# Issuing the products of probabilities and values for two key blocks together in a macaron attention kernel

## The reference, cut to what matters

```python
x = x + 0.5 * ffn(layernorm(x))      # one 128x128 product on inputs rounded to 4-bit floats in blocks of 32
x = x + attn(layernorm(x))           # 16 heads of 8 features, 512 x 512 scores for each head
x = x + 0.5 * ffn(layernorm(x))

def attn(x):
    xq, xk, xv = x @ wq.T + bq, x @ wk.T + bk, x @ wv.T + bv     # then split into heads, rotary on q and k
    scores = einsum('bhqd,bhkd->bhqk', q, k) / sqrt(8)
    return einsum('bhqk,bhkd->bhqd', softmax(scores), v)
```

## Time and profile before

| | us |
|---|---|
| median of 3 runs | 546.12 |
| lowest and highest | 543.88, 546.65 |
| the profiled execution, whole | 543.84 |
| its span, first to last instruction | 542.0 |

### The profile page before, as it was taken

One profiled execution on the slowest core, in us unless ns is written; L12 is line 12 of the kernel. 1 busy time (PEld: TensorE's weight loads), 2 busy tenths in 40 slices (PEclk: granted clock), 3 DMA queues, 4 the chain that ended last, 5 costly groups with the idle time before them and its releaser, 6 DMA issues.

```text
span 542.0 us, 8359 instructions
## 1 busy us (share of the span) xinstructions
PE 455.4 (84%) x2564; PEld 151.8 (28%) x2564; DVE 439.3 (81%) x1004; ACT 380.4 (70%) x746; POOL 228.5 (42%) x336
## 2 busy tenths in 40 slices
PE   2140799999979999999989998999899989998841
PEld 1120232332323332333233222323233323232211
DVE  6636789897999789987998799979997798898125
ACT  6557138687876788687877777878777786777730
POOL 8100047423755365536562665447543624012300
PEclk9985679999999999999999999999999999999995
DMA  5012411231122202231122212210322023200000
GB/s 163 20 48 85 137 41 51 86 95 50 29 91 73 84 31 79 70 101 49 50 89 89 70 51 89 90 66 24 103 74 90 23 76 100 60 2 2 21 1 19
DMA packets 27960, 34.86 MB, mean 64 GB/s; under 512 B 6278, under 2 KB 21260, under 8 KB 27916
## 3 DMA queue, kind: packets, MB, share of 16 engines
q1 hardware_dynamic: 26284, 33.94, 20.3%
q10 hardware_dynamic: 1632, 0.39, 0.3%
HBM read 21.34 MB, written 8.39 MB: 55 GB/s over the span
## 4 chain that ended last, share of the span: by engine, by line
PE 53%; DVE 27%; issue 7%; ACT 6%; POOL 3%; DMA 2%; SPq 1%; POOLq 0%; ACTq 0%; DVEq 0%
PE ot L1105 16%; DVE negmax L882 14%; PE sc L1092 14%; PE st L1081 12%; ACT probs L638 3%; PE misc L1030 3%; PE misc L1047 2%; PE misc L1070 2%; DVE stats_f L751 1%; DVE amax_f L774 1%; ACT feat_k L528 1%; PE misc L1055 1%; PE misc L1025 1%; DMA feat_k<-parts_k 1%; PE misc L1063 1%
## 5 line engine op out<-in xcount | busy, mean ns | idle before, releaser
L882 DVE TENSOR_REDUCE negmax<-sc 128x1 f32<-128x512 f32 x512 | 331.4, 682 | 50.7 <-PE sc L1092 50.1
L638 ACT ACTIVATE probs<-st 128x512 f32<-128x512 f32 x512 | 271.7, 602 | 80.2 <-PE st L1081 78.7
L1092 PE MATMUL sc<-feat_k,feat_q 96*128 96x512 bf16 x512 | 185.3, 391 | 14.7 <-DVE negmax L882 11.7
L1081 PE MATMUL st<-feat_q,feat_k 99*128 99x512 bf16 x512 | 158.1, 380 | 9.6 <-ACT probs L638 8.9
L1105 PE MATMUL ot<-probs,vfeat 128*32 128x512 f32 x1024 | 136.2, 604 | 1.1 <-ACT probs L638 1.0
L1092 PEld LDWEIGHTS sc<-feat_k,feat_q 96*128 96x128 bf16 x512 | 49.7, 97 | 162.3 <-DVE negmax L882 105.7
L1081 PEld LDWEIGHTS st<-feat_q,feat_k 99*128 99x128 bf16 x512 | 49.3, 98 | 82.6 <-ACT probs L638 55.9
L1014 PE MATMUL misc<-identb,xq_f 128*128 128x128 bf16 x64 | 6.8, 235 | 36.9 <-DVE xq_f L826 36.5
L406 POOL TENSOR_TENSOR rstd_f<-ve_f,nhalf 128x4 f32<-128x4 f32 x16 | 16.5, 1034 | 40.8 <-DVE nm_f L763 40.7
L447 POOL TENSOR_SCALAR maxparts<-negmax 128x16 bf16<-128x16 f32 x32 | 8.3, 258 | 57.6 <-DVE negmax L882 57.6
L1105 PEld LDWEIGHTS ot<-probs,vfeat 128*32 128x32 f32 x1024 | 20.2, 108 | 37.5 <-ACT probs L638 23.7
(11 more groups left out here) (134 smaller groups left out, 468.8 us busy)
## 6 DMA issues: line engine op xcount, KB each, us to landing
feat_q<-parts_q SPq DMA_DIRECT2D x96, 96.0 KB
feat_k<-parts_k SPq DMA_DIRECT2D x96, 96.0 KB
qkswap<-qkpre SPq DMA_DIRECT2D x32, 128.0 KB, 2.0
parts_q<-qkparts_q SPq DMA_DIRECT2D x24, 128.0 KB, 2.3
parts_k<-qkparts_k SPq DMA_DIRECT2D x24, 128.0 KB, 2.3
xres<-in_L_attn_x_dram SPq DMA_DIRECT2D x8, 256.0 KB, 5.5
out_dram<-xres SPq DMA_DIRECT2D x8, 256.0 KB, 2.5
feat_q<-maxrows ACTq DMA_DIRECT2D x32, 12.0 KB
```

Source lines behind the costliest of these rows:

```text
L638: nc.scalar.activation(probs[:, s % US, j * S:(j + 1) * S], st[:, bank(2 * s + j), :], ACT.Exp, scale=SCALE).then_inc(exp_done, 1)
L882: nc.vector.tensor_reduce(negmax[:, g, j:j + 1], sc[:, bank(16 * g + j), :], AX.X, ALU.max, negate=True).then_inc(sc_maxed, 1)
L1081: nc.tensor.matmul(st[:, bank(2 * s + j), :], feat["k"][par][0:MROWS, h, kb * P:(kb + 1) * P], feat["q"][par][0:MROWS, h, :], start=True, ...
L1092: nc.tensor.matmul(sc[:, bank(16 * g + j), :], feat["q"][par][0:SROWS, h, t * P:(t + 1) * P], feat["k"][par][0:SROWS, h, :], start=True, s ...
```

## The change

`times_v` is called twice in a row in every fourth step, in place of once in every second: in step 3 of a unit for key blocks 2 and 3 of the unit before, in step 7 for key blocks 0 and 1 of the present unit. Key blocks 2 move from step 1 to step 3, and key blocks 0 from step 5 to step 7; blocks 3 and 1 stay. The matmuls, their operands and their order among themselves are the same, and so are all waits.

```diff
             def slot(b, par):
                 for s in range(STEPS):
                     mb, mpar, mg, ms = ahead(b, par, s)
-                    if s % 2 == 1:
-                        kb = (s % US // 2 + 2) % T
-                        vb, vpar, vg = unit_from(b, par, s // US, -1 if kb >= 2 else 0)
+                    if s % 4 == 3:
+                        half = s % US // 4 ^ 1
+                        vb, vpar, vg = unit_from(b, par, s // US, -half)
                         if has(vb):
-                            times_v(vb, vpar, vg, kb)
+                            times_v(vb, vpar, vg, 2 * half)
+                            times_v(vb, vpar, vg, 2 * half + 1)
                     if has(mb):
                         scores(mb, mpar, mg, 2 * ms)
```

## The result

The changed kernel takes 576.56 us (median of 4 runs, 576.16 to 577.63) against 545.09 for the kernel before on the same chip; the ratio is 1.058, with a 95% interval from 1.055 to 1.061. The forecast was 564.5 with a range of 548 to 576. The direction was right, the size was not: the profiled spans differ by 575.1 - 542.0 = 33.1 us where the sum had said 18.6.

A forecast was written before the change was run, and what follows sets the result against it. No engine alone was taken as the bound: TensorE, VectorE and ScalarE couple through two three-bank queues. Six full batches at +2.4 us (14.6) plus 4 for the last two gave +18.6, forecast 564.5 us, range 548 to 576.

The forecast's parts named there:

- TensorE's saving of 0.23 us a merge: Each joining of two `times_v` blocks removes 0.23 us of TensorE; 63 of them, 14.5 us if all on the path.
- The sign that I gave for it: TensorE's busy time in the profile after would be lower, by some 10 us or more.
- The bare cycle, +0.2: Four-step stretch without other work: later `sc` matmuls wait for maxima to free banks, 5.88 us instead of 5.68.
- Cycles 1, 3, 4, 6, 7 and 8: Four-step stretches of a middle batch: 1 and 7 unchanged, 3 +0.87, 4 -0.45, 6 +0.65, 8 +0.1 us.
- Cycle 5: Fifth four-step stretch: `sc` of step 22 waits for a maximum behind four `stats`, 7.06 against 6.40 us, +0.65.
- Cycle 2, +0.6: Second four-step stretch: the whole double block follows the wait for `turn_max`, 7.66 against 7.05 us.
- Batches 6 and 7, +4: Last two batches, no projections ahead and fewer feed-forward steps: 16 cycles lose about 0.25 us each, 4 us.
- The rival "slower by more": Every cycle's block finds both readers empty and their idle times add, up to +30: 576 us; within slower's 0.83 chance.
- The rival "faster": Each merge's 0.23 us lies on the path and readers keep up: 531.6 us, or 538.9 for half; chance 0.10.
- The rival "no change": Losses of cycles 2, 3, 5 and 6 are partly given back in the next cycle and cancel: 546 us; chance 0.07.

The follow-up runs named there:

- the light kernels: Kernels before and after, each with maxima and exponentials taken of 256 of 512 columns: 527.62 us (before) and 538.68 us (after).
- four repeats: Kernel after with the second `sc` matmul of step 9 issued five times instead of once: 572.26 us, ratio 1.053.
- the step moved: Kernel after with GpSimd's third part of k in step 9 instead of 8: 568.31 us, ratio 1.045; with repeated matmuls as well, 568.04 us.

## Why the prediction was right in direction and wrong in size

- **TensorE's saving of 0.23 us a merge**: right. It appears in full in the light kernels' cycles 1 and 7 and bare cycle (0.24 each), and nearly nowhere in the real ones. It was never the question. The sign that I gave for it was wrong: busy time rose by 8.6 us. A matmul's record counts 0.38 where the next one follows after 0.22 and is overlapped, and in full where a wait follows, so more waits mean more busy time; and a fallen clock lengthens the records (the block of cycle 2 has 3.18 for 1.92).
- **The bare cycle, +0.2**: right in size (5.67 to 5.85), and by the waits that were worked out: the eighth `sc` comes 3.68 after the first (3.71 worked out), and VectorE stands idle 0.92 for the next one (0.83 worked out); the rows stand below. Its explanation, that the block outlasts what three banks hold, was too narrow: two half blocks with three matmuls between them are worse (6.09). The recurrence with banks and paces was right, my one-sentence summary of it was not.

```profile
494.72 0.39 PE L1092 MATMUL sc<-feat_k,feat_q 96*128 96x512 bf16 x1
...
498.40 0.38 PE L1092 MATMUL sc<-feat_k,feat_q 96*128 96x512 bf16 x1
...
501.00 0.69 DVE L882 TENSOR_REDUCE negmax<-sc 128x1 f32<-128x512 f32 x1 [0.92 <-PE sc L1092]
```

- **Cycles 1, 3, 4, 6, 7 and 8**: right within 0.06. Cycle 5: 7.06 worked out, 7.25 measured; no run looks into why.
- **Cycle 2, +0.6**: the step that failed. It measured +2.5 in batches 3 to 5 and +2.9 in batches 1 and 2. Over batches 0 to 5 the cycle grew by 56.70 - 42.97 = 13.7 us where I had 3.6. The queue itself was right: with both disturbances gone the cycle is 7.60, and I had 7.66. Two terms were missing, both put at nothing without a reason given. First, `ve_f` shifted onto GpSimd's instruction and was held until that ended: 0.68 (7.60 without it, 8.28 with it). Second, the granted clock fell: 1.26 for each fall of 3.4 us (8.28 without, 9.54 with). 7.60 + 0.68 + 1.26 = 9.54 is no proof, since both terms are differences of the same three lengths, and the 8.28 holds four repeats, which cost 0.24 in the run with the step moved. But the records give the same prices by themselves: `ve_f` takes 0.85 instead of 0.17, and the block 3.11 instead of 1.86. Nor are the two independent: with the step moved, the clock no longer fell in this cycle. The prediction took all durations from the kernel before and did not ask whether a stretch with more waiting keeps its clock, nor what an instruction that moves by half a microsecond newly meets.
- **Batches 6 and 7, +4**: 6.6 measured (52.6 to 56.2 for batch 6, and 65.0 to 68.0 from the first matmul of batch 7 to the end). I had taken them as light; cycles 2 and 3 lose 0.8 to 0.9 there in each, and cycle 4 of batch 6 loses 1.15.
- 10.1 for cycle 2 and 2.6 for the last batches are 12.7 of the 14.5 us between sum and profile. The rest is small terms: cycle 5 (1.0), what lies ahead of cycle 2 of batch 0 (1.0), cycle 3 (0.2), less 0.6 in cycle 4.
- **The rival "slower by more"** (576) was reached, but not by its mechanism: idle times did not add up in the way it said; the clock and the hold-up did it.
- **The rival "faster"** is refuted for this kernel, and shown for the cycles of the light pair in which only the readers' pace had been in the way; the whole light pair is slower all the same.
- **The rival "no change"**, by refunds, is real in one place: cycle 4 returns 0.65 of the 0.86 that cycle 3 takes. Cycle 3 returns nothing of what cycle 2 takes; the other cycles were not merged one by one.

## What to carry to other kernels

Where engines meet through few buffers and each is busy nine tenths of the time, grouping work to save its borders pays only if it neither makes the supply uneven nor takes work out of a wait that it had filled; the recurrence of starts and bank releases, worked for each stretch, gave seven of eight lengths within 0.2 us. The better move was the reverse one, single blocks put into the waits, though it brought only 0.5%. After any shift of this kind, ask two more questions that durations of the kernel before cannot answer: does TensorE stay busy enough to keep its clock, and which small VectorE instruction now runs into a GpSimd one.

## What the runs showed of the hardware

- TensorE's clock fell to 0.50 behind a stretch whose longest single idle time was 0.82 us, after TensorE had been busy 1.90 of 3.43 us; with the repeats in the same stretch (busy 2.71 of 3.44 us) it stayed at 1.00. Not every such stretch brings a fall, and what decides is open. The Trainium skill, "TensorE: Matmul & The Clock Gate", section "A second HAM failure mode: psum-queue depth-cycling", says of another kernel that cycles through PSUM banks that short idles between groups of matmuls came often enough to make the clock go down and up; the trace agrees. Work that computes nothing new, put into the waits, took 1.26 us off the cycle (9.54 to 8.28); on the whole time the gain is not clear of noise (572.26 against 576.56, on two chips).
- VectorE's instructions on four columns (`ve_f`, `nm_f`), 0.16 to 0.17 us alone, take up to 1.16 when GpSimd's `tensor_tensor` runs, and end 20 to 30 ns after it; the 0.85 of `ve_f` in the kernel after and the 1.16 of `nm_f` in batch 1 of the kernel before are two cases. The Trainium skill, "SBUF — State Buffer", section "SBUF: two separate sides", says of the port pair that VectorE and GpSimd share that it is locked for a whole instruction and the other "fully blocks"; the trace agrees. A maximum that reads PSUM (`negmax`) runs beside the same GpSimd instructions at its usual 0.68; none of the 512 took more than 0.69 in either kernel.
- Sixteen of these 32-column matmuls in a row cost 1.86 us at the full clock and 3.11 where it fell.
- In the kernel before, the next matmul starts 0.22 us after an `sc` matmul where it uses the full width (`st`, `sc`, lines 1038, 1047 and 1070), and 0.31 or more where it has only 3 rows or only 32 or 48 columns (lines 1025, 1052, 1105 and 1063). This bears out the price at the border that the prediction took from one place.
